# Storing block results eight blocks behind the loads, with the row number kept in its register

## The reference

```python
def _L1_ffn_ref(x, router_w, w1, w2, w3):          # x: 1354 x 128, E = 8, H = 341
    probs = jax.nn.softmax(flat @ router_w.T, axis=-1)
    topk_probs, topk_idx = jax.lax.top_k(probs, 2)
    ...
    h1 = jnp.einsum('nc,ehc->neh', flat, w1)
    h3 = jnp.einsum('nc,ehc->neh', flat, w3)
    h = jax.nn.silu(h1) * h3
    y = jnp.einsum('neh,ech->nec', h, w2)
    out = jnp.einsum('ne,nec->nc', gates, y)
```

## Time and profile before

| | |
|---|---|
| median of 3 runs | 669.05 us (668.02 to 670.05) |
| the profiled execution: its own time | 672.23 us |
| its span, first to last instruction | 670.4 us |
| PE busy | 502.2 us (75%) |
| DVE busy | 348.8 us (52%) |
| ACT busy | 240.0 us (36%) |
| POOL busy | 55.4 us (8%) |
| mean granted TensorE clock | 0.853 |

### The profile page before, as it was taken

The page is one execution under the profiler, slowest core; times in us unless marked ns, Lnnn a source line. Parts: engine busy times, 40 slices in busy tenths (PEclk is TensorE's granted clock), DMA queues, the critical chain, the costliest instruction groups (busy, mean ns, idle before and its releaser), DMA issues.

```text
span 670.4 us, 6670 instructions
## 1 busy us (share of the span) xinstructions
PE 502.2 (75%) x1856; PEld 297.8 (44%) x1858; DVE 348.8 (52%) x757; ACT 240.0 (36%) x390; POOL 55.4 (8%) x97
## 2 busy tenths in 40 slices
PE   5586887979999998999999977666656667666800
PEld 3334444535654555444434545444544445444600
DVE  2989887848653267489687685523411122111202
ACT  5977868767532122412221222351111111111200
POOL 4000000001000000000000040400300400000052
PEclk9796999979999989999999978776787657666765
DMA  8989200000000000000340010100100100000021
GB/s 289 314 335 414 106 0 1 0 1 0 1 0 1 0 2 1 0 1 23 97 135 21 0 43 5 37 23 20 41 25 23 48 24 16 25 23 23 22 62 43
DMA packets 29521, 37.67 MB, mean 56 GB/s; under 512 B 3998, under 2 KB 22891, under 8 KB 29479
## 3 DMA queue, kind: packets, MB, share of 16 engines
q1 hardware_dynamic: 27815, 34.39, 15.0%
q0 software_dynamic: 1664, 2.78, 1.5%
HBM read 19.35 MB, written 17.81 MB: 55 GB/s over the span
## 4 chain that ended last, share of the span: by engine, by line
PE 42%; DVE 20%; issue 11%; DMA 9%; ACT 8%; SPq 7%; POOL 3%; another core or an unknown queue 0%; POOLq 0%; DVEq 0%; ACTq 0%
DMA xblk<-xg 8%; PE bank L1262 8%; PE bank L1340 6%; PE bank L1084 3%; PE bank L1210 3%; PE bank L1333 2%; DVE pr_ring L1958 2%; SPq L440 2%; SPq L446 2%; SPq L447 2%; PE bank L1318 2%; PE bank L1251 2%; POOL picked_y L548 2%; PE bank L1171 2%; DVE y_units L1448 2%
## 5 line engine op out<-in xcount | busy, mean ns | idle before, releaser
L1262 PE MATMUL bank<-pr_ring,hW 128*128 128x512 f32 (+3 forms) x198 | 94.1, 561 | 7.8 <-DVE pr_ring L1958 6.5
L1958 DVE SCALAR_TENSOR_TENSOR pr_ring<-adjT,regR,bank 128x512 f32<-128x512 f32 (+3 forms) x99 | 64.8, 679 | 31.6 <-PE bank L1251 30.0
L1318 PE MATMUL bank<-ident,xblk 128*128 128x128 f32 x36 | 14.0, 388 | 68.5 <-DMA xblk<-xg 63.9
L844 ACT COPY hturned<-bank 114x384 f32<-114x384 f32 x36 | 17.2, 479 | 102.9 <-PE bank L1333 98.1
L1262 PEld LDWEIGHTS bank<-pr_ring,hW 128*128 128x128 f32 (+1 forms) x198 | 35.0, 194 | 36.9 <-issue 17.6
L1992 DVE TENSOR_TENSOR hbuf<-hbuf,bank 128x341 f32<-128x341 f32 x36 | 18.3, 509 | 59.3 <-PE bank L1327 49.4
L1318 PEld LDWEIGHTS bank<-ident,xblk 128*128 128x128 f32 x36 | 5.9, 165 | 91.6 <-DMA xblk<-xg 86.1
L934 PE MATMUL bank<-y_units,msg 128*128 128x512 f32 (+3 forms) x66 | 32.0, 614 | 19.1 <-DVE y_units L1469 19.1
L1340 PE MATMUL bank<-wall,hturned 114*128 (+1 forms) x216 | 45.4, 370 | 0.7 <-DVE yblk L1980 0.6
L1326 PE MATMUL bank<-wall,xturned 128*128 x72 | 44.6, 718 | 1.2 <-issue 0.6
L1045 PE MATMUL bank<-hr_ring,W2s 128*128 128x512 f32 (+1 forms) x96 | 44.3, 548 | 0.0
(11 more groups left out here) (303 smaller groups left out, 939.0 us busy)
## 6 DMA issues: line engine op xcount, KB each, us to landing
xg<-zeros SPq DMA_DIRECT2D x1, 4032.0 KB, 24.5
yg<-zeros SPq DMA_DIRECT2D x1, 4032.0 KB, 32.6
wall<-in_w SPq DMA_DIRECT2D x2, 1364.0 KB
adjT<-in_adjT SPq DMA_DIRECT2D x1, 2560.0 KB
xg<-zeros SPq DMA_DIRECT2D x1, 2496.0 KB, 10.4
yg<-zeros SPq DMA_DIRECT2D x1, 2496.0 KB, 15.8
xblk<-xg SPq DMA_DIRECT2D x36, 64.0 KB, 1.8
yg<-yblk SPq DMA_DIRECT2D x36, 64.0 KB, 1.5
```

The lines of the kernel that those rows point to most:

```text
L1262: nc.tensor.matmul(B_ACC[:, 0:w], hW[0:r, j, k * P:(k + 1) * P], ring[0:r, 0:w], start=(k == 0 and j == 0), stop=(k == K - 1 and j == T - ...
L1318: nc.tensor.transpose(B_X[:, 0:P], xblk[:, b % XRING, :], ident[:, :]).then_inc(s["xt_ps"], 1)
L1958: nc.vector.scalar_tensor_tensor(out=pr_ring[0:r, 4 + p % R_RING, 0:w], in0=adjT[0:r, j, cols(c)], scalar=g_col[0:r, j, k:k + 1], in1=B_F[ ...
```

## The change

`HOLD` goes from 4 to 8, and the row number that the load read is kept in a Python dictionary of register values, `starts`, until the store takes it. The rings keep their 4 buffers each.

```diff
 XRING = 4
 YRING = 4
-HOLD = 4
+HOLD = 8
...
+            starts = {}
+
             def block_load(b):
                 g, i = BLOCK[b]
                 if i == 0:
...
                 at(sp, "xt_ps", b - XRING + 1)
                 row = sp.value_load(row_no[0:1, b:b + 1], min_val=0, max_val=(TABLE[g] - 1) * P)
+                starts[b] = row
                 sp.dma_start(xblk[:, b % XRING, :], xg_d[g][bass.ds(row, P), :]).then_inc(s[f"xb_in{b % XRING}"], 16)
 
             def block_store(b):
                 g = BLOCK[b][0]
                 sp.wait_ge(s["y_set"], b + 1)
-                row = sp.value_load(row_no[0:1, b:b + 1], min_val=0, max_val=(TABLE[g] - 1) * P)
+                row = starts.pop(b)
                 sp.dma_start(yg_d[g][bass.ds(row, P), :], yblk[:, b % YRING, :]).then_inc(s[f"y_out{b % YRING}"], 16)
 
             for b in range(NB):
                 block_load(b)
                 if b >= HOLD:
                     block_store(b - HOLD)
             for b in range(NB - HOLD, NB):
                 block_store(b)
```

## The result

The changed kernel takes 572.15 us (median of 4 runs, 568.73 to 575.32), the kernel before 669.55 (4 runs, 668.02 to 670.12). The ratio is 0.855, with a 95% interval of 0.849 to 0.860. The profiled execution took 575.32 us for itself, over a span of 573.6.

What follows compares the result with a forecast made beforehand. The prediction took a closed loop of load, transpose, `down`, `block_out` and store as the bound. Gains of 14.1, 13.8, 69.8 and 2.4, together 100.1, took 672.2 to 572.1 us, so about 570; 8-in-10 range 557 to 603.

Steps and rivals of the forecast that it cites:

- the loop: Load, transpose, `down`, `block_out`, store, next load in the blocks: 6.25 us per block before, PE alone needing 2.25.
- ring: `yblk` ring: stores come too late for its 4 buffers, making the kernel slower than before, 714 us; chance 0.02.
- 436 us to the first scatter: Early blocks: five load waits of 10.7 us go, plus half of 6.8 from the clock; gain 14.1.
- First scatter to block 15's transpose: Block 15 waiting on group 1's scatters: 27.1 us before, 13.3 after; gain 13.8.
- Block 15's to block 35's transpose: Twenty blocks: 125.4 us before, 55.6 after, from 45.0 plus 7.2 stall and 3.4 clock; gain 69.8.
- PE's stall: Up to block 23's transpose, PE is held behind DVE's wait for group 0's gathers: 7.2 us, 6.2 by the shorter landing.
- DVE's wait: Before group 0's combine in iteration 19, DVE waits 8.4 us for the gathered rows.
- To the last store: From block 35's transpose: clock relapse of 1.7 us and last row number of 0.7 go; gain 2.4, tail unchanged.
- Two relapses of the clock: After block 15's wait and the group 0 combine stall, half clock costs 1.7 us each, 3.4 in all.
- they add nothing: Stores of blocks 7 to 10, queued behind block 15's load, cost no time: `block_out(11)` is wanted about when released.
- rival 1: Clock stays low or swings in the blocks: 590 us at 0.67, 618 at 0.50 throughout; chance 0.12.
- rival 2: A hop or PE's sequencer sets the block period, 2.6 to 3.0 us: 578 to 590 us; chance 0.15.

Runs made afterwards that it cites:

- c1: The changed kernel again, unedited, as the measure of its own set on another chip: 569.05 us, ratio 0.858.
- set A: Kernels run together on one chip: row number kept at distance 4, distance 8 with number read twice, distance 6, combine later; ratios 0.954, 0.862, 0.858, 0.860.
- hold 4: The changed kernel with HOLD back at 4, the row number still kept in a register: 635.5 us, ratio 0.954.
- hold 6: The changed kernel with HOLD 6 in place of 8, row number kept: 571.14 us, ratio 0.858.
- set B: Kernels run together on one chip: changed kernel again, before with PE kept busy, group 0's gathers last, gathers in pairs; ratios 0.858, 0.974, 0.860, 0.848.
- set C: Kernels run together on one chip: two result buffers, gathers in pairs with later combine again, the same with HOLD 6; ratios 0.863, 0.846, 0.848.

## Why the prediction was right

The forecast was 570 us, the median is 572.15; for the profiled execution 572.1 against 575.32. (572.1 less 3.2 is 568.9, so the forecast was rounded up by 1.1.) The likeliest case came, by its mechanism: the loop opened, and neither clock, sequencer nor ring took its place. By its own terms:

1. **436 us to the first scatter**: gain 12.0 (462.29 in place of 474.34), predicted 14.1. The blocks began 1.6 us later in this execution (first `up` at 427.05, before 425.46), which is most of the difference. The 1.6 does not belong to the change: in c1, the same kernel, they began at 425.43 and the first scatter came at 459.41, a gain of 14.9, on another chip.
2. **First scatter to block 15's transpose**: 462.29 to 475.53 is 13.2, predicted 13.3.
3. **Block 15's to block 35's transpose**: 475.53 to 531.44 is 55.9, predicted 55.6. PE's stall was 6.96 (predicted 7.2), DVE's wait 8.23 (8.4), the period 2.26 (2.25), and a relapse of the clock came, with the products of `up` at 1.35 in place of 0.74.
4. **To the last store**: gain 2.5, predicted 2.4. The tail, assumed unchanged, was 1.0 longer (540.70 to 573.6, before 638.55 to 670.4).

Three parts of term 3 were right in sum only. Two relapses of the clock were counted at 1.7 each, one of them behind block 15's wait, which was to be about 2 us. That wait was 0.5 and the clock stayed at 1.00 behind it; the one relapse that came, from 501.53 to 508.86, made two periods 2.8 us longer together. The landing of group 0's last gather, taken as 3.83, was 2.2, the lower side. And "they add nothing", said of the stores queued behind block 15's load, was wrong by some 2 us: SP issues a load and a store in 1.58 us and was still catching up when block 14's result was ready at 484.49.

```profile
484.20 0.29 DVE L1983 COPY yblk<-bank 128x128 f32<-128x128 f32 x1 [0.33 <-PE bank L1343]
...
486.19 0.38 SPq L450 DMA_DIRECT2D yg<-yblk  x1
...
497.49 0.94 POOL L551 DMA_INDIRECT picked_y<-yg,slot  x1 [0.30 <-issue]
```

The three rows are block 14's result, its store and the last gather. The store went out 1.7 us after the result, with no wait left but the queue. The landing 1.6 shorter and the backlog 1.7 longer cancelled.

The stall itself can have a second cause, which the prediction does not name. The late gathers do hold DVE, and in c1 they are the whole of it. In set A, with that wait gone, the late starts while POOL issues its transfers cost about as much, 6.87 at the worst. That the forecast of the stall's size held there is luck: both causes lie over the same stretch. A forecast of the gain from the later combine was made, 9 to 10 us, and it was wrong by nearly all of that.

The rivals: the clock was 1.00 in the steady stretch, so rival 1 fell, and with it, here, the rule of the Trainium skill ("TensorE: Matmul & The Clock Gate", section "A second HAM failure mode: psum-queue depth-cycling"). The blocks use five banks in each iteration, seven over two, and each third of the stretch from 508 to 532 us is at 1.00. But the small gaps that the rule speaks of were not there either: PE is busy for all 24 us, so a case with such gaps was not tested. The period of 2.26 leaves nothing for rival 2. SP's waits for `block_out` stayed, 26.9 us in 23, and cost nothing, as forecast.

## What to carry to other kernels

When a queue carries both what feeds an engine and what its results release, look for the closed loop in that queue's waits and count how many blocks lie between the two: here four more blocks of distance brought 92 us with no new buffer, and 31 us came from four short instructions less inside the loop, what the clock added included. Cost the loop and the clock apart, since filling the idle engine with work that nothing reads shows the clock's share (18 us of 97). Before a wait is counted as the only cause of a stall, look in the same stretch for starts that nothing released: one of 4.81 us stood in the trace of before, and an experiment that removed the wait showed that such starts can be worth as much. And repeat the kernel itself beside each set of experiments: c1 shows that late starts seen in one set can be missing in another.

## What the hardware did that I had not expected

- While POOL issues six or eight indirect transfers some 1.25 us apart, instructions on ACT and DVE can start up to 6.87 us late with nothing in the profile that held them. Between the gathers of group 0 they came in the profiled executions of the kernel before (4.81), of the changed kernel (3.15), and of those with hold 4 (3.04), with hold 6 (4.31), with the later combine (6.87) and with two result buffers (5.7); they did not come in c1's or in that with the number read twice, where the combine held DVE for 7.1 and 13.5 us. They also stand beside the scatters: ACT's copy to `x3tok` started 2.82 us late in the changed kernel and 4.4 with hold 6. No such start marked "remote" stands before 420 us in any profile, and none at all in the four of set B. With pauses between pairs of gathers two kernels of set C had none between the gathers. Why they come, and why not in set B, is not shown. The Trainium skill ("Runtime: NRT & Kernel Launch", section "Instruction fetch mechanics") says that each sequencer fetches its instructions by transfers of its own; that fetches come late behind the gathers' packets would fit that several engines are held at once. The traces do not bear this out: the queues that the profile calls "instruction" moved no packet from 493 to 499 us in the kernel with the later combine, and none from 520 to 541 us in the kernel before. Whether these queues show every engine's fetches is not known, so the cause stays open.
- Sixteen transposes per block that nothing reads, in PE's idle time, raised the granted clock from 0.66 to 1.00 and made a kernel with more work 18 us faster.
- The same 64 KB transfer from `yblk` landed 1.57 us after its issue for block 14's store, against 2.61 for the last of the program; the last gather of group 0 landed after 2.21, that of group 1 after 4.01.
